# Twelve-stage kernel on one core: wider convolution operations, a sixth tap on TensorE, and local attention's preparation woven into the state space stage

## The chip, the cores and the metric

The kernel runs on one core of a Trainium2 chip. The metric is the device time of one execution in microseconds, less is better. The kernel before takes 2621.99 us (median of three runs, 2620.91 to 2624.01).

## The reference, cut to what matters

A chain of layers on x of 32 sequences x 128 positions x 128 features, float32. The first two layers touch the change:

```python
x = x + attn0(gru(cond, x))        # GRU, then a Mamba-2 state space block
x = x + ffn0(local_attn(x, cond))  # cond2: 16 heads, each position sees itself,
                                   # its two neighbours and one key made of cond
x = x + attn1(lstm(x, cond)); x = x + ffn1(lstm(x, cond))

# in attn0: 384 channels, causal depthwise convolution of 16 taps, then silu
zxbcdt = x @ W_in
xBC = silu(conv(zxbcdt[..., 256:640], conv_w, 16 taps) + conv_b)
# scan over positions with decay exp(dt * A), gate by silu(z), RMS norm, W_out, W_nl

# in local_attn: q = x WQ + bQ, k = x WK + bK, ak = cond WK + bK, av = cond WV + bV
# scores over [ak, k(t-1), k(t), k(t+1)], softmax, values [av, k(t-1), k(t), k(t+1)], WO
```

## The kernel before

The kernel is one program of five in-order instruction streams (PE, ACT, DVE, POOL, SP), written out by hand. Every method `xxx_pe`, `xxx_act`, `xxx_dve`, `xxx_pool` is a generator, and `weave` (L60) runs several of them turn by turn: at each turn a lane emits what stands before its next `yield`. So the order on each engine is fixed by the number of yields; `wait_ge` on named semaphores is all that holds an engine back.

The stages are the GRU (to about 318 us), the state space stage (to 763 us), the preparation of local attention (`cprep_*`, to about 797 us), local attention (`cond2_*`), a mixture of experts, and three more.

**State space stage.** Four lanes are woven (L217, L227, L237): `mdt_*` (step sizes, at the start), `mamba_*(0)` and `mamba_*(1)`, two workers that take alternate units of four sequences (four units each, n = 0 to 15 counts a worker's sequences), and `conv_*`, which goes ahead of both. `MAMBA_UNIT_TURNS` starts worker 0 eight turns in and worker 1 at turn 22, so worker 0 ends first. The convolution works on 24 tiles of 128 channels x 512 columns (4 sequences x 128 positions). For a tile, PE projects into bank 6, ACT copies it to `XP` (`conv.x`), PE does the first `NT` = 5 taps as products with diagonal matrices `tap` into bank 7 (`conv.taps`), ACT moves bank 7 to the accumulator with the bias (`conv.b`), and DVE adds taps 5 to 15 (L704 and on), each as two operations of 256 columns:

```python
for k in range(NT, 16):
    for i in range(2):
        b2 = slice(2 * i, 2 * i + 2)
        if k > NT:
            e.wait_ge(*at("conv.acc", n, k - 1, i))
        last = stt(e, acc[:, b2, :], X[:, b2, 1 + k:129 + k], self.cw[:, c, k:k + 1], acc[:, b2, :],
                   ALU.mult, ALU.add)
```

An operation waits for the same half's tap before it, and the other half stands between the two. Then ACT does a tanh and DVE the silu product (`silu`), before the next tile's taps.

A worker's sequence n: ACT makes the decays E, PE sums them (`lo`, `B<-catt,low`), ACT exponentiates, PE makes the gate product (`z`, `B<-win,G`) and `bc` (`cross`), DVE makes `cbm`, `xdt` and `e` (L956 to L964), PE makes y (`B<-dg`, `B<-h0T`, then 32 pairs `B<-work,catt`), DVE scales and gates y (L972 to L976). After four sequences: norm (L982, L111), transposes (L827), `W_out` (`B<-work,wout`), a square root and a reciprocal of 128x512 (L992), `W_nl` (`B<-work,wnl`), the sum into X (L106), and POOL adds G (L1006, semaphore `mw{wk}.pool`).

**Preparation** (L1051 to L1150). All engines wait for both workers (`mamba_end`). ACT's queue loads WK and WQ, SP's loads WV and WO (512 KB each). PE makes keys and values of the condition (16 products of 32 columns, `akv`), DVE adds biases, PE multiplies the values by WO (`av`), ACT copies out, SP rearranges it in 16 transfers (`avo`), PE transposes WQ (8 transposes), ACT copies (`wqT`), PE makes `Gak` and `cak`, ACT copies both, then ACT and DVE split WQ and WK into two parts each (`wqk`). Local attention starts when `cak` and the last split are there.

Of the kernel before, what the change touches and what calls it, by code (L numbers as in the profile page):

```python
# [137 lines left out]
NT = 5  # L138
# [23 lines left out]
class Kernel:  # L162
# [51 lines left out]
    def tensor(self, e):  # L214
        self.load_pe(e)
        weave(self.gru_pe(e), self.mprep_pe(e))
        weave((self.mdt_pe(e), 2), self.mamba_pe(e, 0), self.mamba_pe(e, 1), self.conv_pe(e))  # L217
        self.cprep_pe(e)
        weave(self.cond2_pe(e, 0), self.cond2_pe(e, 1))
        self.mix_pe(e, 0)  # L220
        self.attn_pe(e)
        self.mix_pe(e, 1)

    def scalar(self, e):
        self.load_act(e)
        weave(self.gru_act(e), self.mprep_act(e))
        weave((self.mdt_act(e), 2), self.mamba_act(e, 0), self.mamba_act(e, 1), self.conv_act(e))  # L227
        self.cprep_act(e)
# [5 lines left out]
    def vector(self, e):  # L234
        self.load_dve(e)
        weave(self.gru_dve(e), self.mprep_dve(e))
        weave((self.mdt_dve(e), 2), self.mamba_dve(e, 0), self.mamba_dve(e, 1), self.conv_dve(e))  # L237
        self.cprep_dve(e)
# [5 lines left out]
    def gpsimd(self, e):  # L244
# [3 lines left out]
        self.cprep_pool(e)  # L248
# [226 lines left out]
    def lay_mamba(self):  # L475
# [24 lines left out]
        for wk in range(2):  # L500
            wc = [self.catt, wk * 3072]
            m = {"E": [self.area(wc, [128, 8, 128]) for _ in range(2)], "z": [self.area(wc, [128, 256]) for _ in range(2)]}
            m |= {"xdt": ar(128, 256), "cbm": ar(128, 128), "y4": ar(128, 4, 256), "sq": ar(128, 256),
# [181 lines left out]
    def conv_dve(self, e):  # L685
# [17 lines left out]
        for u in range(8):  # L703
            for c in range(3):  # L704
# [5 lines left out]
                for k in range(NT, 16):  # L710
                    for i in range(2):
                        b2 = slice(2 * i, 2 * i + 2)
                        if k > NT:
                            e.wait_ge(*at("conv.acc", n, k - 1, i))
                        last = stt(e, acc[:, b2, :], X[:, b2, 1 + k:129 + k], self.cw[:, c, k:k + 1], acc[:, b2, :],
                                   ALU.mult, ALU.add)
                        last.then_inc(*(inc("conv.acc", n, k, i) if (k, i) != (15, 1) else inc("conv.acc", n)))
# [284 lines left out]
    def mamba_pool(self, e, wk):  # L1002
        for i in range(4):
# [3 lines left out]
                *self.inc(f"mw{wk}.pool", "X", i))  # L1007
            yield
# [3 lines left out]
    def lay_cond2(self):  # L1012
# [11 lines left out]
        w = [self.work, 54 * 256]  # L1024
# [5 lines left out]
        self.avt = self.area([self.work, 8416], [64, 8, 128])  # L1030
# [42 lines left out]
    def cprep_pool(self, e):  # L1073
        self.mamba_end(e)
# [3 lines left out]
    def cprep_pe(self, e):  # L1078
        at, inc = self.at, self.inc
        B0, B1 = self.bank[0:2]  # L1080
        self.mamba_end(e)
        e.wait_ge(*at("ld.cw1"))
        e.wait_ge(*at("ld.cw2"))
        for c in range(8):
            mm(e, B0[:, c * 32:c * 32 + 32], self.WK[:, c, :], self.condT[:], True, True)
            last = mm(e, B0[:, 256 + c * 32:288 + c * 32], self.WV[:, c, :], self.condT[:], True, True)
        last.then_inc(*inc("cprep.pe", "akv"))
        e.wait_ge(*at("cprep.dve", "akv"))
        e.wait_ge(*at("ld.cw4"))
        for g in range(2):  # L1090
            for i in range(4):
                c = 4 * g + i
                last = mm(e, self.bank[g][0:64, i * 128:i * 128 + 128], self.avb[:, c].rearrange("p i b -> p (i b)"),
                          self.WO[:, c, :], True, True)
            last.then_inc(*inc("cprep.pe", "av", g))
        e.wait_ge(*at("ld.cw3"))
        for g in range(2):
            e.wait_ge(*(at("cprep.act", "wq", 0) if g else at("cprep.act", "av", 1)))
            for i in range(4):
                last = e.transpose(B1[:, i * 128:i * 128 + 128], self.WQ[:, 4 * g + i, :], self.ident[:])  # L1100
            last.then_inc(*inc("cprep.pe", "wq", g))
        e.wait_ge(*at("cprep.act", "wq", 1))
        for c in range(8):
            last = mm(e, B0[:, c * 64:c * 64 + 64], self.wqT[:, c, :], self.akb[:, c].rearrange("p i b -> p (i b)"),
                      True, True)
        last.then_inc(*inc("cprep.pe", "Gak"))
        e.wait_ge(*at("cprep.dve", "bqb"))
        for c in range(8):
            last = mm(e, B1[:, c * 64:c * 64 + 64], self.bqb[:, c, :], self.akb[:, c].rearrange("p i b -> p (i b)"),
                      True, True)  # L1110
        last.then_inc(*inc("cprep.pe", "cak"))

# [1267 lines left out]
```

## Time and profile before

| | us |
|---|---|
| median of three runs | 2621.99 |
| the profiled execution | 2625.01 |
| its span | 2623.3 |
| PE busy | 2242.7 (85%) |
| DVE busy | 1861.5 (71%) |
| ACT busy | 1075.2 (41%) |
| POOL busy | 307.6 (12%) |

The profile is of one execution; busy time of an engine is the sum over its instructions without overlaps. A stage's bound is read from the stage: the shares over the whole span mix stages with different limits. Times in the views are microseconds from the span's start.

### The profile page before, as it was taken

What the parts mean: (1) busy time and instruction counts of PE and PEld (TensorE: products, weight loads), DVE (VectorE), ACT (ScalarE), POOL (GpSimd) and SP (SyncE); (2) the same over time, 40 slices, a digit from 0 to 9 for tenths busy, and PEclk for the clock granted to TensorE, in tenths of its full rate; (3) what the DMA queues carried; (4) which work ended last, traced back from release to release, by engine and by line L of the source; (5) the groups of instructions that cost most, each with busy time, mean ns of one, the idle gap of its engine ahead of it and who ended that gap; (6) DMA issues with size and microseconds to landing.
All of it is one profiled execution on the core that took longest, in us unless ns stands there. A gap on an engine that the chain in (4) does not pass through costs nothing.

```text
span 2623.3 us, 60013 instructions
## 1 busy us (share of the span) xinstructions
PE 2242.7 (85%) x24431; PEld 1567.4 (60%) x24489; DVE 1861.5 (71%) x4540; ACT 1075.2 (41%) x2825; POOL 307.6 (12%) x535
## 2 busy tenths in 40 slices
PE   6777778888858888897899999985888789999988
PEld 4555534444436455452588788873555568888855
DVE  4444499999836766775877777733888767777776
ACT  2222145555522111111555555542444345555544
POOL 1111000000001422434000000043322000000000
PEclk6555589998867878786899999987999989999999
DMA  2000000000010000001211111105453111111111
GB/s 52 2 2 2 1 1 1 1 1 1 2 34 14 2 2 2 2 3 42 71 37 33 33 37 33 33 3 102 94 97 70 57 34 37 37 38 37 37 46 32
DMA packets 76052, 76.54 MB, mean 29 GB/s; under 512 B 15768, under 2 KB 57072, under 8 KB 74192
## 3 DMA queue, kind: packets, MB, share of 16 engines
q1 hardware_dynamic: 71872, 70.21, 10.5%
q8 instruction: 192, 3.15, 0.5%
q10 hardware_dynamic: 3904, 2.49, 0.4%
q14 instruction: 84, 0.69, 0.1%
HBM read 60.19 MB, written 11.82 MB: 27 GB/s over the span
## 4 chain that ended last, share of the span: by engine, by line
PE 34%; DVE 10%; ACT 6%; issue 4%; DMA 2%; ACTq 1%; SPq 0%; POOL 0%; DVEq 0%; POOLq 0%
PE B L84 33%; DVE work L1952 2%; ACT hr L102 2%; DMA work<-work 1%; DVE work L106 1%; ACT L102 1%; ACT catt L102 1%; DVE catt L2253 1%; DVE work L1956 1%; ACT work L102 1%; DVE catt L2237 1%; ACTq L2224 1%; ACT lth L102 1%; DMA work<-scr 1%; DVE work L116 1%
## 5 line engine op out<-in xcount | busy, mean ns | idle before, releaser
L84 PE MATMUL B<-gr,wres 128*128 128x512 f32 x1248 | 368.8, 425 | 25.9 <-DVE work L106 13.7
L102 ACT ACTIVATE work<-B 128x512 f32<-128x512 f32 (+5 forms) x460 | 235.2, 530 | 165.7 <-PE B L84 107.3
L84 PEld LDWEIGHTS B<-G,lw 128*128 128x128 f32 (+1 forms) x3256 | 259.9, 178 | 69.2 <-DVE G L106 54.1
L84 PEld LDWEIGHTS B<-gr,wres 128*128 128x128 f32 x1248 | 235.9, 195 | 91.0 <-DVE work L106 28.9
L84 PE MATMUL B<-G,lw 128*128 128x32 f32 (+1 forms) x3256 | 265.2, 304 | 28.5 <-DVE G L106 27.0
L84 PE MATMUL B<-work 128*128 128x128 bf16 (+2 forms) x1360 | 245.0, 307 | 45.4 <-DMA work<-scr 15.1
L102 ACT ACTIVATE hr<-work 128x512 fp32r<-128x512 f32 x272 | 175.7, 646 | 133.0 <-DVE work L106 81.6
L102 ACT ACTIVATE lth<-B 128x96 f32<-128x96 f32 (+1 forms) x512 | 106.0, 227 | 277.5 <-PE B L84 277.4
L84 PEld LDWEIGHTS B<-work 128*128 128x128 bf16 (+1 forms) x1360 | 135.7, 128 | 139.5 <-issue 75.8
L106 DVE SCALAR_TENSOR_TENSOR work<-work,cw 128x256 f32<-128x256 f32 x528 | 214.4, 475 | 0.0
L1952 DVE TENSOR_TENSOR work<-work 128x512 f32<-128x512 f32 x256 | 177.4, 693 | 52.0 <-ACT work L102 45.5
L1943 DVE TENSOR_TENSOR hr<-work,hr 128x512 fp32r<-128x512 f32 x272 | 188.0, 691 | 35.2 <-ACT hr L102 35.0
L106 DVE SCALAR_TENSOR_TENSOR work<-B,ckc,work 128x512 f32<-128x512 f32 x192 | 139.6, 744 | 55.4 <-PE B L84 51.1
L84 PE MATMUL B<-hr,wres 128*128 128x512 f32 x624 | 178.6, 395 | 0.3 <-DVE hr L1943 0.3
L84 PE MATMUL B<-X,lw 128*128 128x128 f32 x512 | 168.6, 420 | 0.0
L1392 DVE TENSOR_TENSOR work<-B,work 128x512 f32<-128x512 f32 x192 | 128.4, 682 | 51.4 <-PE B L84 50.3
L106 DVE SCALAR_TENSOR_TENSOR G<-lth,ltc 128x32 f32<-128x32 f32 x256 | 56.0, 219 | 121.0 <-ACT ltc L102 121.0
L102 ACT ACTIVATE catt<-catt 128x512 f32<-128x512 f32 (+3 forms) x153 | 85.7, 574 | 125.7 <-DVE catt L2237 96.9
L84 PE MATMUL B<-gr,hr 128*128 128x512 f32 x384 | 135.7, 499 | 1.1 <-DVE gr L1332 1.1
L84 PEld LDWEIGHTS B<-hr,wres 128*128 128x128 f32 x624 | 118.4, 190 | 26.7 <-DVE hr L1943 0.7
L102 ACT ACTIVATE work<-B,ckc 128x512 f32<-128x512 f32 x64 | 44.0, 688 | 218.3 <-PE B L84 218.3
L84 PE MATMUL B<-gr,wr 128*128 128x512 f32 x384 | 119.7, 443 | 14.3 <-DVE work L1956 6.8
(253 smaller groups left out, 3865.0 us busy)
## 6 DMA issues: line engine op xcount, KB each, us to landing
work<-wdr SPq DMA_DIRECT2D x128, 256.0 KB, 3.1
scr<-catt SPq DMA_DIRECT2D x144, 64.0 KB, 2.1
work<-scr SPq DMA_DIRECT2D x16, 384.0 KB
work<-scr SPq DMA_DIRECT2D x16, 192.0 KB
catt<-in_L_ffn_ew SPq DMA_DIRECT2D x24, 128.0 KB, 2.3
work<-scr SPq DMA_DIRECT2D x16, 128.0 KB
out<-work SPq DMA_DIRECT2D x32, 64.0 KB, 2.2
work<-in_x ACTq DMA_DIRECT2D x2, 512.0 KB, 5.2
```

The source lines that it names most:

```text
L84: return e.matmul(out, lhsT, rhs, start=start, stop=stop, skip_group_check=True)
L102: return e.activation(out, in_, func, bias=bias, scale=scale)
L106: return e.scalar_tensor_tensor(out=out, in0=a, scalar=s, in1=b, op0=op0, op1=op1)
L116: return e.tensor_reduce(out, a, axis=AX.X, op=op)
L1392: e.tensor_tensor(four(pr[n % 5]), four(B[:]), KP[:, c, :, j:j + 128], ALU.mult).then_inc(*inc(dve, "v", i, c, j))
L1943: e.tensor_tensor(hr[1][:], self.hh[j % 4], hr[0][:].bitcast(F32), ALU.subtract).then_inc(*inc("m.dve", "h", li, j))
L1952: e.tensor_tensor(src, self.sg[i], self.Wb[n % 4], ALU.mult).then_inc(*inc("m.dve", "pu", li, k))
L1956: h = stt(e, self.hh[m], U, 0.5, src, ALU.mult, ALU.mult) if li else e.tensor_tensor(self.hh[m], U, src, ALU.mult)
L2224: e.dma_start(self.aQ[u % 4][48 + q:49 + q, :, :], self.anT[16 * q:16 * q + 16, :]).then_inc(*self.dma("at.max", u))
L2237: e.tensor_tensor(self.aP[n2 % 4].rearrange("p h q -> p (h q)"), B2[n2 % 2][:], self.bT[:, 4 * g:4 * g + 4, :].rearrange("p h q -> p (h q) ...
L2253: then(e, e.reciprocal(self.arc, B[:, 256:512]), "at.dve", "rc", u)
```

## The change

Three edits. One: a DVE tap is one operation of 512 columns that waits for the tap before it. Two: `NT` goes from 5 to 6, so PE makes six taps of a tile and DVE ten (three more diagonal matrices are made in the GRU stage, and `sq` moves to another tile for the room). Three: the preparation becomes generators that are chained behind worker 0's lane, so that its instructions stand between those of worker 1's last sequences; it waits for worker 0 and the last convolution tile (`mamba_first_end`), its buffers move to parts of `work` that only these use, and the copies of `Gak` and `cak` and the 16 transfers stay behind `mamba_end`. POOL's second memset of local attention also waits for the transfers.

```diff
-NT = 5
+NT = 6
@@ tensor (scalar and vector alike)
-        weave((self.mdt_pe(e), 2), self.mamba_pe(e, 0), self.mamba_pe(e, 1), self.conv_pe(e))
-        self.cprep_pe(e)
+        weave((self.mdt_pe(e), 2), chain(self.mamba_pe(e, 0), self.cprep_pe(e)), self.mamba_pe(e, 1), self.conv_pe(e))
         weave(self.cond2_pe(e, 0), self.cond2_pe(e, 1))
@@ conv_dve
                 for k in range(NT, 16):
-                    for i in range(2):
...
+                    if k > NT:
+                        e.wait_ge(*at("conv.acc", n, k - 1))
+                    stt(e, acc, X[:, :, 1 + k:129 + k], self.cw[:, c, k:k + 1], acc, ALU.mult, ALU.add).then_inc(
+                        *(inc("conv.acc", n, k) if k < 15 else inc("conv.acc", n)))
@@ mamba_pool
+            if (wk, i) == (0, 3):
+                self.cprep_pool(e)
@@
+    def mamba_first_end(self, e):
+
+        e.wait_ge(*self.at("mw0.pool", "X", 3))
+        e.wait_ge(*self.at("conv.silu", 23))
@@ cprep_sp
         e.wait_ge(*self.at("cprep.act", "av", 1))
+        self.mamba_end(e)
@@ cprep_pe
-        self.mamba_end(e)
+        yield
+        self.mamba_first_end(e)
         e.wait_ge(*at("ld.cw1"))
         e.wait_ge(*at("ld.cw2"))
...
         last.then_inc(*inc("cprep.pe", "akv"))
+        e.wait_ge(*at("ld.cw3"))
+        for g in range(2):
+            for i in range(4):
+                last = e.transpose(bank[6 + g][:, i * 128:i * 128 + 128], self.WQ[:, 4 * g + i, :], self.ident[:])
+            last.then_inc(*inc("cprep.pe", "wq", g))
+        yield
+        yield
         e.wait_ge(*at("cprep.dve", "akv"))
@@ cprep_act, cprep_dve: the same work with yields between its parts; ACT's last two copies now
+    def cprep_end_act(self, e):
+
+        self.mamba_end(e)
         for B, x, name in ((self.bank[0], self.Gak, "Gak"), (self.bank[1], self.cak, "cak")):
@@ cond2_pool
         if wk:
             e.wait_ge(*at("cprep.act", "cak"))
+            e.wait_ge(*at("cprep.avo"))
```

**DVE, one convolution tile beside a worker's norm** (`work<-work,cw` is a tap, `work<-work` the silu product, L111 the norm). Before:

```order
L106 SCALAR_TENSOR_TENSOR work<-work,cw 128x256 [waits s_conv.acc] x6
L106 SCALAR_TENSOR_TENSOR work<-work 128x512 [waits s_conv.th]
L106 SCALAR_TENSOR_TENSOR work<-work,cw 128x256 [waits s_conv.b]
L106 SCALAR_TENSOR_TENSOR work<-work,cw 128x256
L106 SCALAR_TENSOR_TENSOR work<-work,cw 128x256 [waits s_conv.acc] x2
```

With the change:

```order
L107 SCALAR_TENSOR_TENSOR work<-work,cw 128x512 [waits s_conv.acc] x3
L107 SCALAR_TENSOR_TENSOR work<-work 128x512 [waits s_conv.th]
L107 SCALAR_TENSOR_TENSOR work<-work,cw 128x512 [waits s_conv.b]
```

A group of six halves became three whole taps; behind `conv.b` there were two taps (four halves), now one. Over the stage 528 operations in 75 unbroken runs became 240 in 75 runs: 165 follow the tap that they wait for directly, and 75 end a run.

**PE, from worker 0's last product (`work,wnl`) on** (B3 to B5 are worker 1's banks). Before:

```order
L84 MATMUL B1<-work,wnl 128x512 [waits s_mw0.dve]
L84 MATMUL B4<-catt,low 128x512 [waits s_mw1.dve,s_mw1.act]
...
L84 MATMUL B3<-work,catt 32x32 x31
L84 MATMUL B4<-win,G 128x256 [waits s_mw1.act]
L84 MATMUL B5<-work 128x128 [waits s_mw1.act]
L769 MATMUL B5<-ident,work 128x128 x2
L84 MATMUL B3<-dg,work 128x128 [waits s_mw1.dve]
```

With the change:

```order
L85 MATMUL B3<-work,catt 32x32 x31
L85 MATMUL B0<-condT,catt 128x32 [waits s_ld.cw1,s_ld.cw2,s_conv.silu,s_mw0.pool]
...
L1095 MATMUL B7<-ident,catt 128x128 x4
L85 MATMUL B4<-win,G 128x256 [waits s_mw1.act]
L85 MATMUL B5<-work 128x128 [waits s_mw1.act]
L764 MATMUL B5<-ident,work 128x128 x2
L85 MATMUL B1<-catt,work 64x128 [waits s_ld.cw4,s_cprep.dve]
L85 MATMUL B1<-catt,work 64x128 x3
L85 MATMUL B2<-catt,work 64x128 x4
L85 MATMUL B3<-dg,work 128x128 [waits s_mw1.dve]
```

The key and value products and eight transposes now stand between worker 1's y(14) and gate(15), the `av` products before y(15), and `Gak` and `cak` (16 products) behind y(15), before worker 1's transposes.

**DVE, worker 1's last two sequences, with the change** (L967 to L971 are y, L1165 and L1168 the bias adds and the spread bias, L951 to L959 the products before y, L1175 the split of WQ and WK):

```order
L971 TENSOR_TENSOR work<-work,catt 128x256 [waits s_mw1.dve]
L1165 TENSOR_TENSOR work<-B,ckc 64x8x32 [waits s_cprep.pool,s_ld.cb,s_cprep.pe]
L1165 TENSOR_TENSOR work<-B,cbv 64x8x32
...
L1168 COPY work<-ckc 128x1024
L107 SCALAR_TENSOR_TENSOR catt<-catt,B 128x256 [waits s_mw1.act]
L951 TENSOR_TENSOR work<-B,triq 128x128 [waits s_mw1.pe]
```

Before, the gate (`catt<-catt,B`) followed y(14) directly; the bias adds and the copy stood behind worker 1's last sum into X.

## Rows read from the trace of the kernel before

**Rows 1.** The page: busy time by engine, share of the span.

```profile
PE 2242.7 (85%) x24431; PEld 1567.4 (60%) x24489; DVE 1861.5 (71%) x4540; ACT 1075.2 (41%) x2825; POOL 307.6 (12%) x535
```

**Rows 2.** Windows: busy us (instructions) of PE, PEld, DVE, ACT, POOL; clock, DMA.

```profile
325.00:705.00 380.00, 310.90 (x2540) 155.68 (x2538) 361.68 (x821) 205.07 (x497) 8.84 (x5) 0.92 0.00 1
705.00:763.40 58.40, 39.23 (x413) 20.81 (x412) 30.88 (x57) 26.01 (x60) 3.78 (x3) 0.70 0.00 1
763.40:797.60 34.20, 20.50 (x120) 19.05 (x120) 5.31 (x10) 6.92 (x11) 1.37 (x7) 0.50 0.26 85
```

**Rows 3.** Groups by form, DVE, 325 to 764 us: busy, mean ns | idle.

```profile
L106 DVE SCALAR_TENSOR_TENSOR work<-work,cw 128x256 f32<-128x256 f32 x528 | 214.4, 475 | 0.0
```

**Rows 4.** Waits inside 325 to 705 us: total, times, longest.

```profile
DVE work L106 <- ACT work L102: 13.1, 14, 2.8
...
DVE work L972 <- PE B L84: 0.9, 1, 0.9
```

**Rows 5.** Timeline, DVE, 329 and 486 us: start, duration.

```profile
329.65 8.79 DVE L106 SCALAR_TENSOR_TENSOR work<-work,cw 128x256 f32<-128x256 f32 x22
...
485.66 0.42 DVE L972 TENSOR_TENSOR work<-B,catt 128x256 f32<-128x256 f32 x1
486.12 0.42 DVE L975 TENSOR_TENSOR work<-work,B 128x256 f32<-128x256 f32 x1
```

**Rows 6.** Timeline, DVE, 813 us: three 512-column operations on one bank.

```profile
813.44 2.07 DVE L106 SCALAR_TENSOR_TENSOR work<-B,ckc,work 128x512 f32<-128x512 f32 x3 [1.47 <-ACT work L102]
```

**Rows 7.** Timeline, PE: taps at full and, after 603 us, at half clock.

```profile
454.59 4.47 PE L84 MATMUL B<-work 128*128 128x512 f32 x10
...
603.51 4.15 PE L84 MATMUL B<-work 128*128 128x512 f32 x6
```

**Rows 8.** Timeline, DVE and PE, around 568 us: y ready, y read.

```profile
568.18 0.76 PE L84 MATMUL B<-work,catt 128*32 128x32 f32 x64
...
570.53 0.42 DVE L972 TENSOR_TENSOR work<-B,catt 128x256 f32<-128x256 f32 x1
```

**Rows 9.** Timeline, 728 to 763 us: worker 1 on DVE and PE, then POOL.

```profile
741.80 0.42 DVE L972 TENSOR_TENSOR work<-B,catt 128x256 f32<-128x256 f32 x1 [0.86 <-PE B L84]
...
743.71 0.17 DVE L112 TENSOR_SCALAR work<-work 128x4 f32<-128x4 f32 x1 [0.57 <-ACT work L875]
...
737.49 0.70 PE L84 MATMUL B<-win,G 128*128 128x256 f32 x2
...
740.99 0.76 PE L84 MATMUL B<-work,catt 128*32 128x32 f32 x64 [0.94 <-DVE catt L964]
745.90 1.11 PE L827 MATMUL B<-ident,work 128*128 128x128 f32 x4 [4.14 <-DVE work L111]
...
749.56 3.73 PE L84 MATMUL B<-work,wout 128*128 128x512 f32 x4 [0.69 <-ACT work L102]
...
732.17 1.26 POOL L1006 TENSOR_TENSOR X<-X,G 128x512 f32<-128x512 f32 x1 [24.35 <-DVE X L106]
762.15 1.26 POOL L1006 TENSOR_TENSOR X<-X,G 128x512 f32<-128x512 f32 x1 [28.72 <-DVE X L106]
```

**Rows 10.** Timeline, 769 to 798 us: the preparation, then local attention's first products.

```profile
769.22 0.60 PE L84 MATMUL B<-condT,catt 128*128 128x32 f32 x2 [7.94 <-DMA catt<-in_L_cond_WK_w]
...
777.84 3.67 PE L84 MATMUL B<-catt,work 128*64 128x128 f32 x16 [1.62 <-DVE work L1141]
...
784.06 1.11 PE L1100 MATMUL B<-ident,catt 128*128 128x128 f32 x4 [0.69 <-ACT work L102]
...
785.86 7.09 PE L84 MATMUL B<-work 128*128 128x64 f32 x32 [0.69 <-ACT work L102]
...
792.99 1.02 ACT L102 ACTIVATE catt<-B 128x512 f32<-128x512 f32 x1 [2.39 <-PE B L84]
...
793.82 2.17 ACT L102 ACTIVATE hr<-catt 128x512 fp32r<-128x512 f32 x4
...
797.63 4.52 PE L84 MATMUL B<-gr,hr 128*128 128x512 f32 x12
```

More of the change, by code:

```diff
@@ L3 @@
 from contextlib import ExitStack
+from itertools import chain
 import struct
@@ L226, in scalar @@
         weave(self.gru_act(e), self.mprep_act(e))
-        weave((self.mdt_act(e), 2), self.mamba_act(e, 0), self.mamba_act(e, 1), self.conv_act(e))
-        self.cprep_act(e)
+        weave((self.mdt_act(e), 2), chain(self.mamba_act(e, 0), self.cprep_act(e)), self.mamba_act(e, 1), self.conv_act(e))
+        self.cprep_end_act(e)
         weave(self.cond2_act(e, 0), self.cond2_act(e, 1))
@@ L236, in vector @@
         weave(self.gru_dve(e), self.mprep_dve(e))
[L237 to L238 removed]
+        weave((self.mdt_dve(e), 2), chain(self.mamba_dve(e, 0), self.cprep_dve(e)), self.mamba_dve(e, 1), self.conv_dve(e))
         weave(self.cond2_dve(e, 0), self.cond2_dve(e, 1))
@@ L1092, in cprep_pe @@
                 c = 4 * g + i
-                last = mm(e, self.bank[g][0:64, i * 128:i * 128 + 128], self.avb[:, c].rearrange("p i b -> p (i b)"),
+                last = mm(e, bank[1 + g][0:64, i * 128:i * 128 + 128], self.avb[:, c].rearrange("p i b -> p (i b)"),
                           self.WO[:, c, :], True, True)
             last.then_inc(*inc("cprep.pe", "av", g))
[L1096 to L1101, printed above, removed]
+        yield
+        yield
         e.wait_ge(*at("cprep.act", "wq", 1))
         for c in range(8):
-            last = mm(e, B0[:, c * 64:c * 64 + 64], self.wqT[:, c, :], self.akb[:, c].rearrange("p i b -> p (i b)"),
+            last = mm(e, bank[0][:, c * 64:c * 64 + 64], self.wqT[:, c, :], self.akb[:, c].rearrange("p i b -> p (i b)"),
                       True, True)
@@ L1115, in cprep_act, with split @@
         self.cprep_load(e, "scalar")
+        yield
+        yield
+        for g in range(2):
+            e.wait_ge(*at("cprep.pe", "wq", g))
+            act(e, self.wqT[:, 4 * g:4 * g + 4, :].rearrange("p c m -> p (c m)"), self.bank[6 + g][:], ACT.Copy).then_inc(
+                *inc("cprep.act", "wq", g))
+        yield
+        def split(i):
+            for h in range(2):
+                act(e, self.wqk[i][h][0][:], (self.WQ, self.WK)[i][:, 4 * h:4 * h + 4, :].rearrange("p c m -> p (c m)"),
+                    ACT.Copy).then_inc(*inc("cprep.act", "w", i, h))
+        split(0)
+        yield
         for g in range(2):
             e.wait_ge(*at("cprep.pe", "av", g))
[L1118 to L1123 removed]
+            act(e, self.avt[:, 4 * g:4 * g + 4, :].rearrange("p c m -> p (c m)"), self.bank[1 + g][0:64, :],
+                ACT.Copy).then_inc(*inc("cprep.act", "av", g))
+        yield
+        split(1)
+        yield
+    def cprep_end_act(self, e):
+        self.mamba_end(e)
         for B, x, name in ((self.bank[0], self.Gak, "Gak"), (self.bank[1], self.cak, "cak")):
[L1125 removed]
+            e.wait_ge(*self.at("cprep.pe", name))
             act(e, x.rearrange("p b (c i) -> p c i b", c=8), B[:].rearrange("p (c i b) -> p c i b", c=8, i=2),
[L1127 to L1131 removed]
+                ACT.Copy).then_inc(*self.inc("cprep.act", name))
     def cprep_dve(self, e):
         at, inc = self.at, self.inc
+        yield
+        yield
         e.wait_ge(*at("cprep.pe", "akv"))
```

44 lines of the change are left out of this document (15 added, 29 removed).

## Prediction

> **What bounds the kernel now.** I read the page's busy times first: PE is busy for 85% of the span, DVE for 71% [rows 1]. That says nothing of the two stages touched, so next the windows [rows 2]. From 325 to 705 us, while the convolution runs, DVE is busy 361.7 of 380 us (95%) and PE 310.9 (82%): DVE bounds this stretch. From 705 to 763.4 us the convolution is done and no engine is near full: a chain of worker 1's last sequences. From 763.4 to 797.6 us DVE is busy 5.3 us and PE 20.5 us at a clock of 0.50 (1.2 of 2.4 GHz): this is the preparation, a chain of one engine after another, and all 34.2 us are on the path. The waits say what DVE's missing 5% is: 13.1 us for ACT's tanh before the silu product and 0.9 us for y, hardly any for PE [rows 4].
>
> All sums are made against the profiled execution, 2625.0 us (span 2623.3). The median of the runs shown is 2622.0, 3 us less; savings are carried over unchanged. About 0.2%, 5 us, is what a measurement of this kernel can tell from no change.
>
> **Part 1, DVE's taps.** Now: 528 operations of 256 columns, each 475 ns long [rows 3]. They overlap: 22 take 8.79 us [rows 5], so (8.79 - 0.475) / 21 = 0.396 us from start to start. 528 x 0.396 = 209 us. The other half stands between an operation and the one it waits for, so nothing is exposed.
>
> With the change: 240 operations of 512 columns. No row shows a SBUF tap of that size, so it is bounded by its neighbours. Three 512-column operations of the same kind that do not wait for each other take 2.07 us [rows 6]; with 744 ns for one (256 columns more than the 475 ns one, 0.269 us more) that is (2.07 - 0.744) / 2 = 0.663 us from start to start. That is the lower bound. The upper one is a tap that waits for the one just before it: of two such operations of 256 columns the second starts 0.46 us after the first, which lasts 0.42 [rows 5], so 0.04 us come on top of the length: 0.744 + 0.04 = 0.784 us. Both occur: by the order, 165 of the 240 follow the tap that they wait for directly, 75 are followed by something else. 165 x 0.784 + 75 x 0.663 = 129.4 + 49.7 = 179 us. DVE is relieved of **30 us**: about 19 by the tap that it no longer does (24 x 2 x 0.396), 11 by fewer operations. The merge alone gains little, since a pair of halves costs 0.792 us and a waiting whole 0.784.
>
> A rule speaks for more. The Trainium skill ("VectorE: DVE Perf Modes", "The DRAIN you can't avoid") has the next operation start only when the pipe is empty, and says that a semaphore after each costs nothing extra. The rows disagree: operations that don't wait start before the one before them has ended. By that rule every tap would take the shorter interval, and the relief would be 209 - 240 x 0.663 = 50 us; that is a rival below.
>
> **Part 1, PE's sixth tap.** Ten passes (five taps) take 4.47 us at full clock, so a tap is 0.86 us; where the clock is low for part of them six passes take 4.15, or 1.4 a tap [rows 7]. 24 tiles add **20.6 us** to PE. PE has 69 us idle in the stretch [rows 2], because it waits for DVE, so most of it finds room there and runs before DVE needs it. It is not all free: around 568 us y is ready at 568.94 and DVE reads it at 570.53 [rows 8], 1.6 us of slack, with a tile's taps ahead of it on PE. One tap more takes 0.86. DVE comes there some 1.4 us earlier (28 halves of 0.396, 11.1 us, become 13 whole taps in four runs, 9 x 0.784 + 4 x 0.663 = 9.7). So DVE waits about 0.7 us. I take that for six such places, one for each worker's unit that ends in the stretch, 4 us. The 13 us of waiting for tanh stay as they are: acc, tanh, silu is a chain of its own. So the stretch gets shorter by 30 - 4, **26 us**, with ends at 9 (every added tap on the path: 30 - 20.6; less is the rival below) and 30. Three more diagonal matrices in the GRU stage cost 3 x 0.3 us at most; I take 0.5.
>
> **Part 2, what the preparation's move takes off.** From POOL's last sum (762.15 + 1.26 = 763.41) [rows 9] to local attention's first large product at 797.63 [rows 10] are 34.2 us. What must still follow that sum: two copies of 1.02 us (`Gak`, `cak`), and what stood between the end of the second, 794.01, and 797.63, less the four splits of 2.17 us, which come earlier: 1.45 us. Together 3.6 us with 0.1 for the wait. **30.6 us** go. POOL's second memset now waits for the 16 transfers, some 12 us after that sum (they took 10.4 to issue); the second lane of local attention, which waits for it, starts 22 turns behind the first, which are seven pairs of large products, and two pairs take 4.52 us [rows 10]: 16 us at least, so this is covered. Without that cover up to 12 us would be added.
>
> **Part 2, what it puts into worker 1's lane.** Worker 0's last sum ends at 732.17 + 1.26 = 733.43 [rows 9]. The loads start then, on queues that wait for nothing else; from 763.41 to the first product, 769.22, they took 5.8 us [rows 9, 10], so the first product can start at 739.2. PE reaches it at 737.5, where gate(15) started [rows 9], and stands still for 1.7 us; behind this wait are gate(15), `bc` and y(15). Prices at half clock, from the preparation now: key and value products 7.0 us (769.22 to 777.84 - 1.62), `av` 3.67, eight transposes 2 x 1.1, `Gak` and `cak` 7.09 [rows 10]; at full clock half of each.
> At full clock: products to 742.7, transposes to 743.8, so gate(15) is 6.3 us late. DVE's bias adds and copy (2.3 us from 742.7 on) end about when the gate's tanh is there. `av` adds 1.8 - 0.7 between `bc` and y(15): y(15) starts 7.4 us after its 740.99. DVE's last two splits (1.3 us) come between y(15) and the norm, which waited 0.57 us anyway [rows 9]: 8.1 us. `Gak` and `cak` (3.6 us) fit before the transposes, which start 4 us after y(15) [rows 9]. So **+8 us**. At half clock throughout: gate(15) 10.8 late, y(15) 14.2, and `Gak` and `cak` no longer fit: **+17 us**.
> Which? PE was at half clock in the preparation after a wait of 7.9 us for a load [rows 10]; the wait here is 1.7 us, and gate(15) before it ran at full clock (0.70 us for two passes). I take 11, nearer to the full clock, less 2.5 because a PE that has just done `Gak` and `cak` may run `W_out`, now 3.73 us at half clock [rows 9], at full; plus 1 for a slow start of local attention, whose first products ran at full clock [rows 10] behind a busy PE. Net **+9.5 us**, ends 5 and 18.
>
> A rule speaks against this part. The Trainium skill ("TensorE: Matmul & The Clock Gate", "Loop structure matters more than you think") warns of a long wait for a DMA between matmuls, after which PE runs cold. If it held for this short wait, the +17 of the sum above would be the value, and the time 7 us more.
>
> **The sum.** -26 + 0.5 - 30.6 + 9.5 = -46.6 us. 2625.0 - 46.6 = 2578.4 for a profiled execution, 2622.0 - 46.6 = 2575.4 for the median: **2575.5 us**.
>
> **The rivals.**
> - PE becomes the bound beside DVE. For it: it needs 310.9 + 20.6 = 331.5 us in a stretch that shrinks to 354, 94%, in order. Against: DVE waits 1 us for y now [rows 4], and many of PE's microseconds are at half clock and shrink when it idles less. The convolution then gives only the lower end, 9 us: 2622 - 9 + 0.5 - 30.6 + 9.5 = 2592.4. Chance 0.15.
> - The move costs its upper price, every inserted piece serial and slow, 18 instead of 9.5: 2584. Chance 0.15.
> - Waiting for the tap before costs DVE nothing, so all 240 start 0.663 us apart: 209 - 159 = 50 us of relief instead of 30, of which PE, now nearly full, gives back 10: -40 instead of -26, 2561.5. Against it is the 0.46 us of [rows 5]; for it, that this pair is 256 columns wide and of another kind. Chance 0.05. (It is the case that the rule of the DVE page would make.)
> - **Slower.** The sixth tap is on the path and nothing of DVE's relief is. If PE keeps all of its 69 us of waits, because they come from chains through ACT and not from DVE's load, the stretch takes 310.9 + 20.6 + 69 = 400 us, 20 more than now; with the taps at half clock (twice 0.86) 41 more. With the move at its upper price (0.5 - 30.6 + 18 = -12) that is 2622 + 20 or 41 - 12 = 2630 to 2651. It decides once the stretch is 17 us longer than now, which is when DVE's waits in it pass 14 + 30 + 17 = 61 us; they are 14 now [rows 4]. Chance 0.03.
> - The change doesn't do what it says: the preparation's turns would still run behind worker 1. The order excludes it (chance 0): all but the last copies stand before worker 1's last transposes.
>
> **How the numbers follow.** Forecast as above 0.62 (its own range 2566 to 2587), the rivals 0.15, 0.15, 0.05 and 0.03. Of the slower one a third falls near no change. The range from 2558 to 2598 takes in both ends of part 2, the loss of most of part 1 and nearly the third rival. Faster by over 0.2%: 0.96; within 0.2%: 0.02; slower: 0.02.
>
> **What would show it.** In the changed kernel's profile: 240 taps on DVE of about 744 ns, ten in a row in about 7.8 us; the taps' products in passes of 0.43 us; DVE above 90% from 325 us to the convolution's end near 679; POOL's last sum ending near 746 us instead of 763; from there to the first large product of local attention 4 to 5 us instead of 34; the waits of DVE for PE in the convolution under 8 us. It would be wrong if ten taps in a row took under 7 or over 8.5 us, if DVE waited for PE or ACT for tens of microseconds, or if worker 1's y(15) came more than 15 us after y(14)'s end.

## The result and the profile after

The changed kernel takes 2577.89 us (median of 4 runs, 2576.06 to 2579.98), the kernel before on the same chip 2621.45 (4 runs, 2613.13 to 2624.01): ratio 0.9839, 95% interval 0.9816 to 0.9863, 43.6 us less by the medians. The forecast was 2575.5, in a range of 2558 to 2598. The profiled execution took 2577.03 us (span 2575.2), against 2625.01 (2623.3) before.

The page of the changed kernel, busy time by engine:

```profile
PE 2242.6 (87%) x24537; PEld 1564.4 (61%) x24537; DVE 1826.1 (71%) x4255; ACT 1076.7 (42%) x2825; POOL 308.3 (12%) x535
```

Against [rows 1] PE's busy time is the same and DVE's is 35 us less. As before, that tells little. The windows of the changed kernel, cut at the same points of its work as [rows 2] (2.5 us behind the last tap, POOL's last sum, the first large product of local attention), and behind them the stage up to local attention's last value product. Columns as there:

```profile
325.00:684.80 359.80, 318.44 (x2588) 160.35 (x2586) 326.10 (x531) 206.19 (x497) 8.84 (x5) 0.96 0.00 1
684.80:755.90 71.10, 52.90 (x501) 34.82 (x500) 35.68 (x66) 30.02 (x68) 4.78 (x5) 0.72 0.09 31
755.90:759.00 3.10, 0.63 (x32) 0.52 (x32) 0.69 (x1) 2.30 (x3) 0.22 (x2) 0.50 0.07 16
759.00:1177.20 418.20, 370.82 (x7259) 209.39 (x7260) 299.12 (x493) 76.89 (x127) 140.66 (x112) 0.79 0.02 4
```

The stretch of the convolution is 20.2 us shorter (380 to 359.8), the stretch of worker 1's last sequences 12.7 longer (58.4 to 71.1), the preparation's 34.2 us are 3.1. At the first large product of local attention the changed kernel is 797.63 - 759.02 = 38.6 us ahead. The other 9.5 us of this pair of profiles arise behind that product, where only one wait on POOL was changed.

DVE's taps by form, and the first ten in a row on the timeline, which answer to [rows 3] and [rows 5]:

```profile
L107 DVE SCALAR_TENSOR_TENSOR work<-work,cw 128x512 f32<-128x512 f32 x240 | 179.1, 746 | 5.9
...
328.98 7.83 DVE L107 SCALAR_TENSOR_TENSOR work<-work,cw 128x512 f32<-128x512 f32 x10
```

An operation lasts 746 ns, and ten that wait for one another start (7.83 - 0.746) / 9 = 0.787 us apart. Now DVE's waits from 325 to 684.8 us, which answer to [rows 4] (total, times, longest):

```profile
DVE work L107 <- ACT work L103: 21.2, 14, 4.0
DVE work L967 <- PE B L85: 3.4, 6, 0.7
```

The 14 waits for tanh grew from 13.1 to 21.2 us, those for y from 0.9 to 3.4. What holds tanh back is its place on ACT. Here is the longest of these waits, on ACT and then on DVE (`work<-B,cb` is `conv.b` of the next tile, `work<-work` on ACT the tanh):

```profile
339.56 0.69 ACT L103 ACTIVATE work<-B,cb 128x512 f32<-128x512 f32 x1 [1.98 <-PE B L85]
340.15 0.62 ACT L103 ACTIVATE work<-work 128x512 f32<-128x512 f32 x1
...
340.80 0.69 DVE L107 SCALAR_TENSOR_TENSOR work<-work 128x512 f32<-128x512 f32 x1 [3.99 <-ACT work L103]
```

The accumulator had been ready since the last tap, at 336.8 us, but ACT works in order, and the tanh stands behind a copy that waits for PE's six taps (1.98 us; 1.12 for five, before). Of the 14 waits seven are of 0.70 us, the tanh alone. The other seven sum to 16.4 us, where before there were four with 6.2; in all of them the tanh follows `conv.b` without a pause on ACT, and ACT had waited for PE shortly before, for the taps or for a worker's transposes. In three of them ACT's own eight decays (2.4 us) stand between.

Last, worker 1's lane on PE, behind y(14), which answers to [rows 9] and [rows 10]. The first row in it is y(14), L1095 are the transposes of WQ, the 16 products of `catt,work` are `av`, L822 are worker 1's transposes:

```profile
714.50 0.76 PE L85 MATMUL B<-work,catt 128*32 128x32 f32 x64
...
718.52 0.38 PE L85 MATMUL B<-condT,catt 128*128 128x32 f32 x2 [3.25 <-DMA catt<-in_L_cond_WK_w]
...
720.02 0.61 PE L85 MATMUL B<-condT,catt 128*128 128x32 f32 x2
...
724.29 1.95 PE L1095 MATMUL B<-ident,catt 128*128 128x128 f32 x8
726.03 1.06 PE L85 MATMUL B<-win,G 128*128 128x256 f32 x2
...
728.37 3.67 PE L85 MATMUL B<-catt,work 128*64 128x128 f32 x16
...
733.83 0.76 PE L85 MATMUL B<-work,catt 128*32 128x32 f32 x64
734.52 3.79 PE L85 MATMUL B<-work 128*128 128x64 f32 x32
738.74 0.66 PE L822 MATMUL B<-ident,work 128*128 128x128 f32 x4 [0.43 <-DVE work L112]
...
741.95 3.78 PE L85 MATMUL B<-work,wout 128*128 128x512 f32 x4 [0.69 <-ACT work L103]
```

PE stands 3.25 us for the load of WK; then everything up to y(15) runs in one line. The first key and value products run at full clock (0.38 us for two), those from 719.6 us on at half (0.61), and so do the two passes of gate(15), 1.06 us where they took 0.70, and `av`. The granted clock says the same, 0.54 up to 734.5 us and full for the 32 products of `Gak` and `cak` (3.79 us, against 7.09 before); the first four transposes are still at full clock, the output product is at half again (windows, columns as above):

```profile
719.60:734.50 14.90, 14.90 (x124) 12.79 (x123) 5.68 (x11) 5.01 (x11) 0.00 (x0) 0.54 0.06 18
734.50:738.40 3.90, 3.81 (x42) 3.65 (x32) 3.06 (x9) 2.00 (x4) 0.00 (x0) 1.00 0.01 4
```

y(15) starts 18.6 us after y(14) ended. The end of the stage on POOL, ACT and PE:

```profile
754.59 1.26 POOL L1001 TENSOR_TENSOR X<-X,G 128x512 f32<-128x512 f32 x1 [40.29 <-DVE X L107]
755.94 1.88 ACT L103 ACTIVATE catt<-B 128x512 f32<-128x512 f32 x2 [5.06 <-POOL X L1001]
...
757.62 0.62 ACT L103 ACTIVATE gr<-X 128x512 fp32r<-128x512 f32 x1
...
759.02 5.34 PE L85 MATMUL B<-gr,hr 128*128 128x512 f32 x12 [0.52 <-DVE gr L1360]
```

### The profile page after: what moved, and what is told of

The parts are those of the page before. It is cut to its first block, busy times and chain, and to the rows that moved or that the text cites. A ratio compares the mean times of both kernels' runs of the same rounds, so it can differ in the third digit from the quotient of the medians.

```text
span 2575.2 us, 59885 instructions
## 1 busy us (share of the span) xinstructions
PE 2242.6 (87%) x24537; PEld 1564.4 (61%) x24537; DVE 1826.1 (71%) x4255; ACT 1076.7 (42%) x2825; POOL 308.3 (12%) x535
## 4 chain that ended last, share of the span: by engine, by line
PE 34%; DVE 11%; ACT 6%; issue 4%; DMA 3%; ACTq 1%; SPq 0%; POOL 0%; DVEq 0%; POOLq 0%
PE B L85 33%; DVE work L1981 2%; DMA work<-work 2%; ACT hr L103 2%; DVE work L107 2%; ACT L103 1%; DVE catt L2282 1%; ACT catt L103 1%; DVE work L1985 1%; ACT work L103 1%; DVE catt L2266 1%; ACT lth L103 1%; DVE work L117 1%; ACTq L2253 1%; ACT ltc L103 1%
## 5 line engine op out<-in xcount | busy, mean ns | idle before, releaser
L85 PE MATMUL B<-work 128*128 128x128 bf16 (+3 forms) x1408 | 262.5, 314 | 27.4 <-DMA work<-work 14.0
L85 PEld LDWEIGHTS B<-work 128*128 128x128 bf16 (+2 forms) x1408 | 141.9, 127 | 149.3 <-issue 84.3
L107 DVE SCALAR_TENSOR_TENSOR work<-work,cw 128x512 f32<-128x512 f32 x240 | 179.1, 746 | 5.9
```

Of the source, the lines that this page charges most:

```text
L85: return e.matmul(out, lhsT, rhs, start=start, stop=stop, skip_group_check=True)
L107: return e.scalar_tensor_tensor(out=out, in0=a, scalar=s, in1=b, op0=op0, op1=op1)
```

## The experiments

Each kernel was read at the same marks. W0 and W1 are the ends of POOL's last sum of worker 0 and of worker 1, first product is the start of local attention's first large product, last value the start of DVE's last product with the values; all in us of the profiled execution. The kernel before ran beside each group of them, at medians of 2621.45 to 2623.11 us; its row has the runs beside the first group of experiments, and the marks of its only profile. The groups ran on different chips, so across groups the ratios compare better than the medians.

| kernel | median, us (range, runs) | ratio (95%) | W0 | W1 | first product | last value |
|---|---|---|---|---|---|---|
| before | 2623.11 (2611.85 to 2628.61, 13) | | 733.4 | 763.4 | 797.6 | 1222.0 |
| changed | 2577.89 (2576.06 to 2579.98, 4) | 0.9839 (0.9816 to 0.9863) | 713.3 | 755.9 | 759.0 | 1177.2 |
| changed again | 2575.61 (2570.13 to 2588.39, 6) | 0.9829 (0.9801 to 0.9858) | 713.3 | 755.8 | 759.0 | 1183.8 |
| part 1 alone | 2600.17 (2597.38 to 2604.66, 4) | 0.9916 (0.9895 to 0.9937) | 713.2 | 743.2 | 777.5 | 1195.1 |
| part 2 alone | 2601.29 (2596.72 to 2613.18, 6) | 0.9919 (0.9895 to 0.9944) | 731.5 | 770.3 | 773.4 | 1198.7 |
| wide taps alone | 2613.11 (2604.99 to 2615.76, 8) | 0.9966 (0.9949 to 0.9983) | 720.7 | 751.4 | 784.7 | 1211.0 |
| sixth tap alone | 2599.35 (2597.51 to 2605.7, 4) | 0.9916 (0.9893 to 0.9938) | 717.6 | 747.0 | 781.2 | 1198.6 |
| changed, halves | 2585.35 (2581.36 to 2590.58, 4) | 0.9858 (0.9837 to 0.9879) | 717.5 | 758.3 | 761.5 | 1183.6 |
| seven taps on PE | 2580.29 (2577.75 to 2588.74, 6) | 0.9844 (0.9818 to 0.9870) | 715.7 | 756.7 | 759.9 | 1180.7 |
| silu a tap later | 2577.63 (2570.33 to 2578.92, 4) | 0.9822 (0.9801 to 0.9843) | 715.2 | 757.6 | 760.8 | 1177.2 |
| silu a turn later | 2578.71 (2574.38 to 2585.6, 4) | 0.9834 (0.9811 to 0.9857) | 713.8 | 754.4 | 757.5 | 1183.4 |
| early loads | 2574.84 (2570.88 to 2583.49, 5) | 0.9818 (0.9794 to 0.9843) | 709.4 | 749.9 | 753.1 | 1172.4 |
| pieces in gaps | 2572.2 (2564.72 to 2575.28, 5) | 0.9801 (0.9776 to 0.9827) | 710.1 | 743.4 | 746.6 | 1165.2 |
| in gaps, again | 2570.02 (2564.14 to 2572.65, 5) | 0.9807 (0.9792 to 0.9821) | 713.3 | 743.3 | 746.5 | 1160.0 |

**The two parts.** Part 1 alone is the kernel before with the wide taps and the sixth tap:

```diff
-NT = 5
+NT = 6
-                    for i in range(2):
-                        b2 = slice(2 * i, 2 * i + 2)
...
+                    stt(e, acc, X[:, :, 1 + k:129 + k], self.cw[:, c, k:k + 1], acc, ALU.mult, ALU.add).then_inc(
```

> Part 1 alone: six taps on PE and whole taps of 512 columns on DVE, the preparation behind both workers as before. Theory A (DVE relief of 30 us, of which new waits for ACT and PE take 10): POOL's last sum ends 20 us earlier than before (743 instead of 763), local attention's first large product 20 us earlier (777.5), total -20 +-4 us. Theory B (the two parts help each other, so part 1 alone gives clearly less than the 20 us seen in the changed kernel at worker 0's end): -12 us or less. In both local attention (first large product to its last value product, 424.4 us before, 418.2 changed) tells whether its 6 us are of part 2: if they are, it stays 424 here.

Part 2 alone is the changed kernel with `NT = 5` and the two halves put back.

> Part 2 alone: the preparation in worker 0's lane, five taps and halves as before. Theory A: worker 0's last sum at 733.4 as before, worker 1's 12.6 us later than before (776), local attention's first large product 18 us earlier than before (779.2). Total -18 if the rest is untouched, -25 or more if the 6 to 10 us that the changed kernel gained behind local attention's start come from moving the preparation. Theory B (insertion costs less beside a slower convolution): the same, since the convolution has ended by then.

At the first product part 1 gives 20.1 us and part 2 gives 24.2, together 44.3, where both at once gave 38.6; by the medians 23 and 22. Of the 5.7 us between, 1.9 are worker 0's end, which came at 731.5 with the same five taps and halves as before (733.4), and 3.8 the inserted pieces: W1 was expected at 776 and came at 770.3. The timeline of PE in part 2 alone (gate(15), `av`, y(15), the output product):

```profile
745.10 1.06 PE L85 MATMUL B<-win,G 128*128 128x256 f32 x2
...
747.33 1.96 PE L85 MATMUL B<-catt,work 128*64 128x128 f32 x16
...
750.49 0.76 PE L85 MATMUL B<-work,catt 128*32 128x32 f32 x64
...
758.15 1.99 PE L85 MATMUL B<-work,wout 128*128 128x512 f32 x4 [0.69 <-ACT work L103]
```

`av` and the output product run at full clock (1.96 and 1.99 us against 3.67 and 3.78), and W0 to W1 is 38.7 us instead of 42.6. PE had stood 1.48 us for WK, less than half as long; that this is why the clock was full isn't shown, since in the changed kernel with halves it stood 1.53 us and the output product took 3.78.

**Inside part 1.** The wide taps alone, then the sixth tap alone (with halves), both on the kernel before; then the changed kernel with halves, which is the sixth tap and part 2.

> Only the whole taps: 264 operations of 512 columns, five taps on PE. By start-to-start times of 0.787 us behind the tap it waits for (189) and 0.663 at the end of a run (75): 198 us instead of 209, relief 11 us, total -8 to -11. Rival (halves hid the latency, so the merge gains nothing or costs): 0 to +5.

> Only the sixth tap on PE, DVE in halves: 480 operations of 256 columns, relief 19 us on DVE, 20.6 us more on PE. Theory A (PE has room, part is lost to waits): -12 to -17. Rival (PE is co-bound and the tap is mostly on the path): 0 to -6.

> The changed kernel with DVE's taps in halves of 256 columns again (six taps on PE, preparation moved). DVE has 11 us more to do. Theory A (beside six taps on PE the stretch is held by PE and by ACT's tanh as much as by DVE, so the merge gives only the 4.4 us by which the runs of part 1 and of the sixth tap alone differ at worker 0's end): worker 0's last sum at 717.5 instead of 713.3, total +2 to +6 against the changed kernel. Theory B (DVE's work counts in full): +11.

At W0 the wide taps give 12.7 us (11 were worked out) and the sixth tap 15.8 (19 less what y costs). The sum would be 28.5; together they give 20.2. On top of six taps on PE the wide taps bring 4.2 us (717.5 to 713.3), up to 8 if W0 of two other profiles of equal tap code, 709.4 and 710.1, is taken. So 4 to 8 us of relief find nothing to shorten. The whole times don't settle it. In the changed kernel the wide taps are worth 7.5 us by the medians and 5 by the ratios, whose intervals overlap; on the kernel before, on one chip, the sixth tap alone took 2599.35 us and both together 2600.17. The sixth tap alone gave 23.8 us by the medians, where 12 to 17 were expected and W0 gave 15.8.

**Who has become the second bound.** If DVE still bound the stretch alone, a seventh tap on PE would give nearly its whole 19 us again.

```diff
-NT = 6
+NT = 7
-            m |= {"xdt": ar(128, 256), "cbm": ar(128, 128), ...
+            m |= {"xdt": ar(128, 256), "cbm": self.area(c, [128, 128]), ...
...
+                yield
                 e.wait_ge(*at("conv.b", n))
                 for k in range(NT, 16):
```

> The changed kernel with a seventh tap on TensorE (9 whole taps on VectorE instead of 10), which takes 24 operations of 0.787 us, 19 us, from VectorE and adds 24 products of 0.86 us, 20.6 us, to TensorE. Theory A (in the changed kernel TensorE and VectorE bound the stretch of the convolutions together, as the missing 8 us of the two parts of the change say): nothing to win, worker 0's last sum ends within -5 and +5 us of 713.3, median 2573 to 2583. Theory B (VectorE alone is still the bound): worker 0's last sum ends 12 to 17 us earlier, median 2560 to 2566. Theory C (TensorE is already the sole bound): 15 to 20 us later, median 2592 to 2598.

(The added `yield` keeps a tile's turns where they were, now that one tap less is followed by one.) It gives nothing: W0 comes 2.4 us later. Its windows row and DVE's waits in the stretch:

```profile
325.00:684.70 359.70, 326.53 (x2630) 165.36 (x2628) 306.39 (x499) 205.76 (x495) 8.85 (x5) 0.99 0.00 1
```

```profile
DVE work L107 <- ACT work L103: 33.5, 14, 5.6
...
DVE work L968 <- PE B L85: 10.8, 8, 2.8
```

DVE is busy 19.7 us less than in the changed kernel and waits 19.7 us more (24.6 to 44.3): everything it was relieved of came back as waiting. PE is now the fullest engine, busy 91% of the stretch at a clock of 0.99, and ACT's waits for PE, which hold back the tanh behind them, grew from 96 to 116 us (77 in the kernel before). So theory A came true. No engine fills the stretch alone; that PE's work bounds it, and not the order in which ACT does its own, isn't shown: no run puts the tanh ahead of `conv.b` on ACT.

**Moving the wait.** 21.2 us of DVE's waits are for tanh. If the silu product stood one tap later on DVE, tanh would be there:

```diff
-                if n:
-                    silu(n - 1)
                 e.wait_ge(*at("conv.b", n))
...
+                    if k == NT and n:
+                        silu(n - 1)
```

> The changed kernel with the silu product of tile n-1 behind the first tap of tile n, in the same turn, so that DVE has 0.66 us of work while ACT does the tanh. In the changed kernel DVE waits 20.5 us before this product, in 14 places. Theory A (those waits are lost time): they fall by 14 x 0.66 = 9 us, worker 0's end 6 to 9 us earlier. Theory B (ACT comes late there because it waits for PE, so DVE would only wait at the next place): 0 to -3.

> As the run with the silu product behind the first tap, but one turn later still, so that the workers' DVE instructions of that turn stand between too. Theory A: the 20.5 us of waits go nearly all, worker 0's end 12 to 18 us earlier than in the changed kernel. Theory B (PE is busy 318 of 357 us and its order sets the pace): -3 to -6, with DVE's waits moved to its y operations.

DVE's waits in the two (325 to 684.8 us), first silu a tap later, then a turn later:

```profile
DVE work L107 <- ACT work L103: 14.2, 8, 3.5
DVE work L969 <- PE B L85: 11.5, 8, 3.5
```

```profile
DVE work L967 <- PE B L85: 17.3, 8, 4.6
DVE work L107 <- ACT work L103: 11.4, 9, 3.5
```

The waits for tanh fell by 7 and 10 us, those for y rose by 8 and 14; W0 came 1.9 and 0.5 us later. A wait taken from one place turned up at the next result of PE that DVE reads. Neither theory had W0 later; of the two, B had the mechanism.

**The price of the inserted preparation.** First only the loads: issued on SP once y(15) of worker 0 has been read, not after its last sum.

```diff
     def cprep_load(self, e, queue):
-        self.mamba_first_end(e)
+        e.wait_ge(*self.at("mw0.dve", "yz", 15))
+        e.wait_ge(*self.at("mw0.pe", "y", 15))
+        e.wait_ge(*self.at("conv.silu", 23))
```

> The changed kernel with the four weight loads on SP's queue, issued as soon as worker 0 has read its last decays and gate (some 18 us earlier) instead of after its last sum. In the changed kernel PE stood 3.25 us for WK at 718.5, and the key and value products, the first transposes and av then ran at half clock; worker 1's last sum came 42.6 us after worker 0's, 30.0 before. Theory A (the wait and the low clock behind it are 4 to 6 of the 12.6 us): 42.6 goes to 37 to 39, total -3 to -6 against the changed kernel. Theory B (the inserted products themselves are the price, the wait was idle time that would be there anyway): 42 or more, total 0 to -1.

PE no longer stands for WK (the key products start at 714.19, as y(14) ends), but W0 to W1 falls by 2.1 us only, 42.6 to 40.5: the clock was at half speed already (four passes of 512 columns ahead of y(14) took 3.78 us, 1.98 in the changed kernel), and the pieces stayed in one line. That is between the two theories. The wait for WK is no lever anyway: the repeat of the changed kernel stood only 0.95 us for it, because y(14) ended later there, and the key products started at 718.5 and worker 1's sum ended at 755.8 as in the first profile. So next the pieces themselves were moved into the gaps of worker 1's chain:

```diff
     def cprep_pe(self, e):
+        yield
         yield
         self.mamba_first_end(e)
...
         last.then_inc(*inc("cprep.pe", "akv"))
+        yield
+        yield
+        yield
         e.wait_ge(*at("ld.cw3"))
...
-        yield
-        yield
         e.wait_ge(*at("cprep.dve", "akv"))
...
-        yield
-        yield
+        for _ in range(5):
+            yield
         e.wait_ge(*at("cprep.act", "wq", 1))
```

and ACT's and DVE's pieces to match (all four splits of DVE ahead of worker 1's last reciprocal).

> The changed kernel with its whole preparation, but its pieces put where the trace shows each engine standing in worker 1's last turns: the four weight loads issued on SP once y(15) of worker 0 has been read; on TensorE the 16 products of the key and value rows behind gate(15) and cross(15) instead of ahead of them, the transposes of WQ and the products of the output weight behind y(15), the last 16 products between the output product and the large normalisation product; on VectorE the additions behind e(15), the four splits ahead of worker 1's last reciprocal; on ScalarE the splits early, the copies behind the last square. Theory A (the 12.6 us by which the distance from worker 0's last sum to worker 1's grew are the price of this order: TensorE runs 12 us of preparation in one line with the chain gate(15), y(15), transposes): the distance falls from 42.6 us to 31 to 36, worker 1's last sum ends near 745 us instead of 755.9 (749.9 with the loads alone moved), and the first large product starts near 748; median 2564 to 2570. Theory B (TensorE's clock, at half speed there, is what costs: any order pays it, and filling the gaps moves nothing): distance 39 to 42, median 2573 to 2578. If the clock is at full speed in that stretch, the columns of the products say so (under 2.0 us for the group of 16 of the output weight, against 3.7).

> The changed kernel again, unaltered, on the chip of the last runs. It serves two purposes: a median to set beside the rearranged preparation on the same chip (2575 to 2581 us expected), and a second profile, which tells how much of what lies behind the first large product is the execution's and not the kernel's. If the 6 us that local attention lost in the first profiled pair (424.4 to 418.2 us from its first product to its last value product) come from the change, this profile gives 417 to 419 again; if they are the spread of the granted clock, anything from 416 to 426, with worker 0's last sum within 1 us of 713.3 and worker 1's within 2 us of 755.9 all the same.

> The rearranged preparation again, unaltered. Its first profile had the first large product at 746.61 us, 12.4 us before the changed kernel's, but its median over 5 runs was only 3.4 us below the changed kernel's on the same chip, with runs of both spread over 11 to 18 us. Theory A (the stage is shorter by 12 us each time, and the medians differ by less because the granted clock of what follows spreads): the first large product within 1 us of 746.6 again, worker 0's last sum to worker 1's 33 to 34 us, and a median anywhere from 2562 to 2574. Theory B (the gain is lost again behind the stage): the marks as before, but local attention from first product to last value product 5 us or more above the 417 to 426 us of all the other profiles, and a median of 2572 to 2578.

Worker 1's last turns on PE in the first of these profiles (L1102 are the transposes of WQ, the 32 products `Gak` and `cak`):

```profile
714.90 0.70 PE L85 MATMUL B<-win,G 128*128 128x256 f32 x2
...
720.95 0.76 PE L85 MATMUL B<-work,catt 128*32 128x32 f32 x64
721.65 1.09 PE L1102 MATMUL B<-ident,catt 128*128 128x128 f32 x8
722.67 1.96 PE L85 MATMUL B<-catt,work 128*64 128x128 f32 x16
727.28 0.66 PE L822 MATMUL B<-ident,work 128*128 128x128 f32 x4 [2.65 <-DVE work L112]
...
730.48 3.78 PE L85 MATMUL B<-work,wout 128*128 128x512 f32 x4 [0.69 <-ACT work L103]
734.06 4.09 PE L85 MATMUL B<-work 128*128 128x64 f32 x32
740.18 1.12 PE L85 MATMUL B<-work,wnl 128*128 128x512 f32 x2 [2.03 <-DVE work L991]
...
746.61 5.49 PE L85 MATMUL B<-gr,hr 128*128 128x512 f32 x12 [0.52 <-DVE gr L1365]
```

W0 to W1 is 33.3 us (31 to 36 were expected), and 30.0 in the repeat (33 to 34 were expected): as short as in the kernel before, which has no preparation there at all. The first product starts at 746.6 and 746.5, 12.5 us ahead of the changed kernel. Counted from W0, y(15) starts 3.3 and 1.9 us later than in the kernel before, against 13.0 in the changed kernel; that is the order's doing in the main. That the repeat has no price left at all owes 1.8 us to the output product, which ran at full clock there (1.98 us, 3.73 in the kernel before). How much of the 13.0 us is the line and how much its half clock isn't separated: the order changed the clock too. With the loads alone moved, the key and value products ran mostly at full clock and y(15) was still 10.9 us late. In whole time less of it shows: with the runs of both rows of each kernel taken together, ten and ten, the medians are 2576.5 for the changed kernel and 2571.1 for this one, 5.4 us (by the means 7.8). The median beside the first profile, 2572.2, lies above the 2564 to 2570 expected. The version is the fastest of all; whether the missing 5 us are given back behind the stage or are the spread of ten runs is open.

**What lies behind the stage.** Windows from the first product to the last value product, of the changed kernel's second profile and of the last kernel's repeat; the first profile's row stands above:

```profile
759.00:1183.80 424.80, 378.46 (x7259) 213.81 (x7260) 299.87 (x493) 76.80 (x127) 140.67 (x113) 0.77 0.02 4
```

```profile
746.50:1160.00 413.50, 366.75 (x7259) 207.37 (x7260) 298.75 (x493) 76.91 (x127) 140.78 (x112) 0.81 0.02 4
```

The same kernel took 418.2 and 424.8 us here, with all marks before it within 0.1 us: DVE's busy time is the same, PE's is 7.6 us more at a clock of 0.77 against 0.79. Before took 424.4, and all fourteen profiles lie between 413.5 and 426.3: those without the moved preparation at 417.4 to 426.3, those with it at 413.5 to 425.9. The 6.2 us that this stage gained in the first pair, and the 3.3 behind it, are no effect of the change that these runs can show.

## Why the prediction held, and where it didn't

The number was right within 2.4 us; two of its terms were too favourable by 10 us together, and what the pair of executions differed by behind the stage hid it.

- **DVE's taps, 209 to 179 us.** Held: 746 ns a tap (744 forecast), 0.787 us apart (0.784), ten in 7.83 us (7.8). The Trainium skill's sentence in "VectorE: DVE Perf Modes", "The DRAIN you can't avoid", that a semaphore after each costs nothing extra, does not carry over to these taps, each of which also waits for the one before: they start 0.787 us apart where three that don't wait start 0.663 apart [rows 6]. The rival built on it would have had ten taps in 6.7 us; it is out.
- **PE's sixth tap, 30 - 4 = 26 us.** This step failed in size: 20.2 us. I let only the waits for y grow, by 4, and wrote that the 13 us for tanh stay as they are, "a chain of its own". They grew by 8.1 and y's by 2.5, 10.6 together. The tanh stands on ACT behind `conv.b`, which waits for PE's taps, so a fuller PE delays it too. The text's own sign of being wrong, tens of microseconds of waiting for PE or ACT, was met with 24.6. The first rival (PE becomes a bound beside DVE) was right in kind and not in size: it left 9 us of gain, and 20 are there, but the seventh tap shows that with six the point is reached from which more taps on PE give nothing. The end of the convolution was to be near 679, which is 705 less 26; at the same mark it was 684.8. The 0.5 us for three more diagonal matrices had no row behind it and doesn't show: the first tap started at 328.98, before at 329.65.
- **Preparation off the tail, -30.6.** Held: 34.2 us became 3.2 (755.85 to 759.02), 31.0. The copies took 1.88, as 2 x 1.02 less their overlap. POOL's second memset waited 12.8 us for the transfers and delayed nothing that the marks show.
- **Inserted into worker 1's lane, +8.5 at W1 (and 1 for a slow start).** This step failed in size: W0 to W1 grew by 12.6 us, and POOL's last sum ended at 755.9, not near 746. Counted as the forecast counts, from worker 0's last sum, gate(15) came 8.7 us late (6.3 worked out at full clock, 10.8 at half) and y(15) 13.0 (7.4 and 14.2). I took a value nearer to the full clock, and the trace shows half for most of the line. Behind y(15) I credited 2.5 us for an output product at full clock; it took 3.78 us, at half, and only 0.4 came back: `Gak` and `cak` fitted before the transposes, as worked out. In part 2 alone y(15) was 11.4 us late and 2.6 came back, with the output product at 1.99: 8.7 us in all, near the 8.5 forecast. So what was mis-sized is the clock of this stretch. PE stood 3.25 us for WK, not 1.7, but that is no part of the error: y(14) ended earlier, and WK was there 5.3 us behind worker 0's sum, against 5.8 worked out. The text named y(15) more than 15 us after y(14)'s end as a sign that it was wrong, and it came 18.6 after. The slow start was 0.8 us (the first twelve products took 5.34 us, 4.52 before). The Trainium skill's warning of a wait for a DMA ("TensorE: Matmul & The Clock Gate", "Loop structure matters more than you think") agrees in its outcome, half clock behind the wait, but not as the cause: with the loads early PE didn't wait for WK and the clock fell to half all the same (the pairs of key and value products went from 0.39 to 0.61 us at 717.1). The forecast's 7 us more for that case came as 4.
- **The sum.** -20.2 - 31.0 + 12.6 = -38.6 us at the first product, where the same steps had forecast -26 - 30.6 + 8.5 = -48.1. The medians say -43.6 (the interval of the ratio: -36 to -48), -46.1 on another chip. The profiled pair says -48.0, of which 9.5 arise behind the first product. So the match to 2.4 us is partly luck; by the marks alone the time would have been 2583, inside the range.
- **Slower.** Out: DVE's waits in the stretch are 24.6 us, against the 61 from which that rival decides. The seventh tap, which adds as much again to PE, ended worker 0 only 2.4 us later.

## What to carry to other kernels

When work is moved from a full engine to one at 80%, count the chains that pass through the receiving engine as well: here the waits for a third engine grew, because its instructions stand behind ones that wait for the receiving engine, and the gain ended after one step (the seventh tap gave nothing). Of a preparation moved beside a serial chain, the place of each piece decides more than its length: the same products cost 8.7 to 12.6 us in one line with the chain and 0 to 3.3 in its gaps. When a change is worth 1 to 2% here, read it at marks in the trace as well as by the whole time.

## What the runs showed of the hardware

The granted clock at a given product differs between executions of the same kernel: the output product of worker 1 took 3.78 us (half clock) in one profile of the last kernel and 1.98 in the other, and the runs of the changed kernel on one chip were 2570 to 2576 us where the mean clock was 0.869 to 0.870, and 2587 and 2588 us where it was 0.864. Two profiles of equal code up to that point also ended worker 0 at 710.1 and 713.3 us. Neither could be tied to anything in the program.

The clock also fell while PE was working without a break. In the repeat of the last kernel PE is busy for 8.05 of 8.10 us at full clock, and the clock then falls at the last two of the 16 key and value products (two passes of 32 columns each), with no wait in front; PE stays busy throughout:

```profile
711.50:719.60 8.10, 8.05 (x109) 6.15 (x109) 3.71 (x8) 4.45 (x11) 2.25 (x3) 1.00 0.02 4
719.60:727.00 7.40, 7.40 (x93) 6.13 (x93) 3.83 (x10) 1.75 (x5) 0.00 (x0) 0.54 0.00 0
```

In the first profile of that kernel the same products ran at full clock to their end, so this too is one execution's.
